# Where the gated output bias is added: four matmuls per group, or GpSimd on the residual rows

## The chip, the cores and the metric

One core of one Trainium2 chip. The metric is the device time of one execution in microseconds (us); lower is better. All times of operations are read from one profiled execution.

## What is computed

A gated cross-attention block, followed by a mixture of eight experts, on 4 x 1024 rows of width 256:

```
x = x + tanh(g_xattn) * (attention(layernorm(x), ctx) @ w_proj.T + b_proj)
x = x + tanh(g_ffn)   * experts_top2(layernorm(x))
```

The attention has 16 heads of 64 and a context of 64 rows; its result is multiplied by the queries ahead of the projection. `b_proj` is a vector of 256. The change concerns only how `tanh(g_xattn) * b_proj` gets into the first line. The experts (two of eight for each row) read what the first line gives.

## The kernel before

The program has two blocks with a barrier between them: `attention` (about the first 357 us of the span) and `experts`.

**Attention.** The 4096 rows are handled in 8 groups of 512 (NG = 8), each as four tiles of 128 rows (TG = 4), and each group in 8 steps, one for each pair of heads (NP = 8). The steps are a software pipeline written out by hand: every engine has its own `step`, and at step n = 8g + p TensorE does the queries of pair n, the scores of n-1, the transposes of the probabilities of n-4, probabilities times values of n-5 and the output projection of n-6; the other engines do what lies between. So the projection of the last pair of group g-1 is done in step 5 of group g (`project_out`, L644), and its result is added to the residual rows in step 6 of group g (`residual`, L1033, VectorE: `xres = pj_ps * gains + xres`, 128x1024 elements). `gains` is tanh(g)/64, because the weights of the projection are held 64 times too large (WS = 64) as two float16 parts, high and low.

**The bias.** At the start ScalarE and VectorE make `bias_rows`, a 128x256 float16 tile that is zero but for row 0 (64 times the bias, high part) and row 32 (its low part): L938, L786 to L788, L992. For the last pair of each group, TensorE multiplies it with a tile of ones (L659), once per tile of rows: four matmuls of 256 columns per group, 32 in all, accumulated in the same PSUM as the projection.

**Order within a step.** What the prediction speaks of, by engine. TensorE ends step 5 with the first transposes of the next group's normalized rows (`x_transpose`, L547). From group 2 to group 6 these wait for the semaphore `pos_read`, since they use the bank `job_ps` that `pick_rows` (L250, VectorE) reads last. VectorE does the routing of group g-2 in steps 3 to 5 of group g, in the gaps between its attention work: logits, best experts, masks (L229), `delta` (L232), `mboth` (L237), positions, `next_row` (L250). In the last group `early_table` (L1069 to L1101) lies between these too. `expert_lo` (L1067) splits an eighth of one expert's weights per step, behind ScalarE's `expert_hi` (L867). ScalarE normalizes the next group's rows in steps 4 and 5 (`ln1_apply`, L765). GpSimd does, in each step: `normalize` (L1300, output `pn`), small powers or the start of a scatter of the routed rows (L1278, L1314, L1316), then `product_lo` (L1306, output `r_l`), which waits for ScalarE's `r_h` (L832). At the end of the last group LAST = 6 more steps drain the pipeline. There VectorE makes the last two `r_l` itself (L1247) and the rest of a table of blocks (L1112 to L1123).

**Residual rows.** SyncE loads group g's rows of x into `xres[g % 2]` (L467) once the rows of g-2 are stored; the issues lie at 42.2 us for group 0, 55.2 for group 1, 274.6 for group 6 and 316.2 for group 7. `residual` waits for that load.

**Last group.** `residual` of group 7 is done in the experts part, at L1638.

**Experts.** 71 blocks of 128 gathered rows, each through two float16 split matmuls (L1483, L1496), TensorE busy nearly throughout. Nothing of it is changed.

Of the kernel before, what the change touches and what calls it, by code (L numbers as in the profile page):

```python
# [22 lines left out]
F32 = mybir.dt.float32  # L23
F16 = mybir.dt.float16
U32 = mybir.dt.uint32
I32 = mybir.dt.int32
ACT = mybir.ActivationFunctionType
ALU = mybir.AluOpType
AX = mybir.AxisListType

P = 128
B, L, D = 4, 1024, 256
# [4 lines left out]
NP = H // 2  # L37
TG = 4
G = TG * P
NG = T // G  # L40
# [4 lines left out]
WS = 64.0  # L45
# [224 lines left out]
def attention(nc, ctx, dram, carry, weights):  # L270
    ident = carry.ident
    gate_t, ones, before, iota_e, tok_ids, minus_half = (
        carry.gate_t, carry.ones, carry.before, carry.iota_e, carry.tok_ids, carry.minus_half)
    pad_rec, gains, wait_mark = carry.pad_rec, carry.gains, carry.wait_mark
# [4 lines left out]
    def sb(name, shape, dt):  # L279
        return ctx.enter_context(nc.sbuf_tensor(name, shape, dt))  # L280
# [4 lines left out]
    def sem(name):  # L285
        return ctx.enter_context(nc.semaphore(name))
# [3 lines left out]
    wp_h, wp_l = (sb(f"wp_{s}", [P, NP, D], F16) for s in "hl")  # L290
    kb = sb("kb", [P, B, NP, 2 * M], F32)
    vb = sb("vb", [P, B, NP, 2, DK], F32)
    bias_rows = sb("bias_rows", [P, D], F16)
    bias_high = sb("bias_high", [64, D], F16)
    tanhs = sb("tanhs", [P, 2], F32)

    stage = sb("stage", [P, WN], F32)
    split = sb("split", [P, 2, WN], F16)
    bias_sb = sb("bias_sb", [64, D], F32)  # L300

    xin = sb("xin", [P, 2, TG, D], F32)
    xres = carry.x1
# [45 lines left out]
    pj_ps = carry.pair_ps  # L350
# [4 lines left out]
    gain_in, gate_in, bias_in, ctx_in, wk_in, wv_in, wp_in = (sem(n) for n in (  # L355
        "gain_in", "gate_in", "bias_in", "ctx_in", "wk_in", "wv_in", "wp_in"))
# [6 lines left out]
    xres_in = [sem(f"xres_in{i}") for i in range(2)]  # L363
# [1 line left out]
    x1_stored = sem("x1_stored")  # L365
    base_set, consts_set, k_zeroed, setup_ops, tanh_done, first_rows = (sem(n) for n in (
        "base_set", "consts_set", "k_zeroed", "setup_ops", "tanh_done", "first_rows"))
    wp_hi, wp_lo, wq_hi, wq_lo, bias_hi = (sem(n) for n in ("wp_hi", "wp_lo", "wq_hi", "wq_lo", "bias_hi"))
    bias_zeroed, bias_lo = sem("bias_zeroed"), sem("bias_lo")
    k_mm, k_placed, v_mm, v_placed = (sem(n) for n in ("k_mm", "k_placed", "v_mm", "v_placed"))  # L370
    ln1_ops, ln1_rstd, ln1_shift, xn_done, xt_tp, xt_hi, xt_lo = (sem(n) for n in ("ln1_ops", "ln1_rstd", "ln1_shift", "xn_done", "xt_tp", "xt_hi", "xt_lo"))
    last_r_lo = sem("last_r_lo")
# [2 lines left out]
    e_sum, e_inv, p_nrm, ot_mm, r_mul, r_hi, r_lo, pj_mm = (sem(n) for n in (  # L375
        "e_sum", "e_inv", "p_nrm", "ot_mm", "r_mul", "r_hi", "r_lo", "pj_mm"))
# [10 lines left out]
    def pair_no(g, p):  # L387
        return g * NP + p

    def known(g, least):  # L390

        return not isinstance(g, int) or g >= least
# [45 lines left out]
    def _(sp):  # L438
# [1 line left out]
        sp.dma_start(xin[:, 0, TG // 2:TG], x_groups[0][:, TG // 2:TG]).then_inc(x_in[0], 16)  # L440
        sp.dma_start(ctx_t, dram["ctxt"]).then_inc(ctx_in, 16)
        sp.dma_start(wk_sb, dram["wk"]).then_inc(wk_in, 16)
        sp.dma_start(bias_sb[:, :], dram["bproj"].partition_broadcast(64)).then_inc(bias_in, 16)
        sp.dma_start(wv_sb, dram["wv"]).then_inc(wv_in, 16)
        sp.dma_start(wp_sb, dram["wproj"]).then_inc(wp_in, 16)
        sp.dma_start(gate_t[:, :, :], dram["gate"]).then_inc(gate_in, 16)
# [93 lines left out]
    def _(pe):  # L540
# [103 lines left out]
        def project_out(g, n, p):  # L644
            pe.wait_ge(r_hi, n + 1)
            if isinstance(n, int) and n == 0:
                pe.wait_ge(v_placed, B)
                pe.wait_ge(bias_hi, 2)
                pe.wait_ge(bias_lo, 1)
                pe.wait_ge(consts_set, CONSTS)  # L650
            if p == 0:
                after(pe, x1_done, g)
            for t in range(TG):
                for i, wt in enumerate((wp_h, wp_l)):

                    nc.tensor.matmul(pj_ps[:, t, :], r_h[:, p % 2, t * P:(t + 1) * P], wt[:, p, :],  # L656
                                     start=(p == 0 and i == 0 and t % 2 == 0), stop=False, skip_group_check=True)
                if p == NP - 1:
                    nc.tensor.matmul(pj_ps[:, t, :], ones[:, :], bias_rows[:, :], start=False, stop=False, skip_group_check=True)  # L659
            if isinstance(n, int) and n >= NS - 2:  # L660
                pe.wait_ge(last_r_lo, n - NS + 3)
            else:
                pe.wait_ge(r_lo, n + 1)
            for t in range(TG):
                last = nc.tensor.matmul(pj_ps[:, t, :], r_l[:, p % 2, t * P:(t + 1) * P], wp_h[:, p, :],
                                        start=False, stop=(p == NP - 1), skip_group_check=True)
            last.then_inc(pj_mm, 1)
# [75 lines left out]
        for p in range(LAST):  # L743
            n = NS + p
# [9 lines left out]
    def _(act):  # L754
# [27 lines left out]
            split_wq(half)  # L782
        for k in range(KD):
            split_x(0, 0, k, first_banks[k])
        act.wait_ge(bias_in, 16)
        nc.scalar.mul(bias_high[:, :], bias_sb[:, :], WS).then_inc(bias_hi, 1)  # L786
        act.wait_ge(bias_zeroed, 1)
        nc.scalar.mul(bias_rows[0:1, :], bias_sb[0:1, :], WS).then_inc(bias_hi, 1)  # L788

        def place_k(p):  # L790

# [130 lines left out]
        for p in range(LAST):  # L922
            n = NS + p
# [11 lines left out]
    @block.vector  # L935
    def _(dve):
        nc.vector.memset(kb[:, 0:B // 2].rearrange("p b n m -> p (b n m)").bitcast(U32), 0).then_inc(k_zeroed, 1)
        nc.vector.memset(bias_rows[:, :].bitcast(U32), 0).then_inc(bias_zeroed, 1)  # L938

        def ln1(g, par):  # L940

# [45 lines left out]
        for k in range(KD):  # L987
            split_x(0, 0, k, first_banks[k])
        split_wq(1)
        dve.wait_ge(bias_hi, 1)  # L990
        dve.wait_ge(bias_zeroed, 1)
        nc.vector.scalar_tensor_tensor(bias_rows[32:33, :], bias_sb[32:33, :], WS, bias_high[32:33, :],  # L992
                                       ALU.mult, ALU.subtract).then_inc(bias_lo, 1)

        def place_k(p):

# [36 lines left out]
        def residual(g, par):  # L1033

            dve.wait_ge(pj_mm, pair_no(g, NP))
            dve.wait_ge(xres_in[par], 16 * (g // 2) + 16 if isinstance(g, int) else g)
            nc.vector.scalar_tensor_tensor(xres[par][:, :, :], pj_ps[:, :, :], gains[:, 0:1], xres[par][:, :, :],
                                           ALU.mult, ALU.add).then_inc(x1_done, 1)

# [165 lines left out]
            last.then_inc(ln1_ops, 1)  # L1205

        def residual_of(b, g, k):
            if isinstance(b, int):
                residual(g - 1, 1 - k)
                return  # L1210
            par = 1 - k
            dve.wait_ge(pj_mm, pair_no(g - 1, NP))
            dve.wait_ge(xres_in[par], (b + k) * 16)
            nc.vector.scalar_tensor_tensor(xres[par][:, :, :], pj_ps[:, :, :], gains[:, 0:1], xres[par][:, :, :],
                                           ALU.mult, ALU.add).then_inc(x1_done, 1)

        for k in range(GB):
            for p in range(NP):
                step(0, k, k, p, pairs_back=min(LAST, k * NP + p))
            if k == 0:  # L1220
                dve.wait_ge(tanh_done, 1)
                nc.vector.tensor_scalar(carry.halves[:, 0:1], tanhs[:, 1:2], 0.5 / WS, None, ALU.mult)
                nc.vector.tensor_scalar(carry.halves[:, 1:2], tanhs[:, 1:2], -0.5 / WS, None, ALU.mult)
                nc.vector.tensor_scalar(gains[:, :], tanhs[:, :], 1.0 / WS, None, ALU.mult).then_inc(setup_ops, 1)
                dve.wait_ge(setup_ops, 1)
# [7 lines left out]
        for p in range(LAST):  # L1233
            n = NS + p
# [24 lines left out]
    def _(pool):  # L1259
# [43 lines left out]
        def product_lo(n, p):  # L1303

            pool.wait_ge(r_hi, n + 1)
            nc.gpsimd.tensor_tensor(r_l[:, p % 2, :], r32[:, p % 2, :], r_h[:, p % 2, :], ALU.subtract).then_inc(r_lo, 1)  # L1306

        def scatter(g, par, i):

            if i == 0:  # L1310
                pool.wait_ge(routed.slots_done, g + 1)
                pool.wait_ge(rec_done, g + 1)

                nc.gpsimd.tensor_tensor(wait_mark[:, 1:2], wait_mark[:, 0:1], wait_mark[:, 0:1], ALU.add)  # L1314
            c, t = i // TG, i % TG
            pool.indirect_dma_start(records, bass.IndirectOffsetOnAxis(slot[par][:, c, t:t + 1], 0),  # L1316
                                    rec[par][:, c, t, :], None).then_inc(records_in[par], 16)

        def step(g, k, p, pairs_back=LAST):
            n = pair_no(g, p)  # L1320
            if pairs_back >= 3:
                normalize(n - 3, (p - 3) % NP)
            if p == 3 and has_next(g):
                ln_rstd(0, g + 1, ln1_ops, ln1_rstd)
            if p == 7 and known(g, 1) and has_next(g):
                ln_rstd(1, g - 1, ln2_ops, ln2_rstd)
            if p >= 5 and known(g, 2):
                scatter(g - 2, k, p - 5)
            if p < 5 and known(g, 3):
                scatter(g - 3, 1 - k, p + 3)  # L1330
            if pairs_back >= 5:
                product_lo(n - 5, (p - 5) % NP)

        for g in range(GB + 1):
            for p in range(NP):
# [12 lines left out]
        for p in range(NP):  # L1348
            step(NG - 1, 1, p)
        for p in range(3):  # L1350
            normalize(NS + p - 3, NP + p - 3)
            product_lo(NS + p - 5, NP + p - 5)
        pool.wait_ge(records_in[0], 16 + 32 * TG * (B - 1))
        pool.wait_ge(records_in[1], 16 + 32 * TG * (B - 2) + 16 * (2 * TG - LEFT))

# [442 lines left out]
```

## Time and profile before

| What | us |
|---|---|
| Median of 3 runs | 764.19 (764.18 to 774.77) |
| The profiled execution, its own time | 762.03 |
| Its span, first to last instruction | 760.3 |
| TensorE busy in the span | 728.7 |
| VectorE busy | 584.4 |
| ScalarE busy | 377.3 |
| GpSimd busy | 371.3 |

In the profile PE is TensorE's matmuls, PEld its weight loads, DVE VectorE, ACT ScalarE, POOL GpSimd. A row of the timeline gives the start and the duration in us, the engine, the line, output<-inputs and the shape; in square brackets stands the idle time of the engine just before it and what ended that. Matmuls are pipelined, and their listed durations overlap: the distance of two starts is what one costs. L12 is line 12 of the kernel. The granted TensorE clock was 0.997 of full speed in the mean.

### The profile page before, as it was taken

To read this page: it belongs to the slowest core of one execution; us is meant where nothing else is said; L and a number is where in the kernel's file an instruction comes from. 1 tells how busy PE (TensorE), PEld (TensorE's weight loads), DVE (VectorE), ACT (ScalarE), POOL (GpSimd) and SP (SyncE) were. 2 spreads that over 40 slices of the span, in tenths; PEclk is the share of its full clock that TensorE was granted. 3 is DMA by queue.
4 is the path that set the end of the run, shared out by engine and by line. 5 is a ranking of instruction groups with operands and counts; after the bars stand their busy time and mean duration, and the time that the engine had idled before them with its cause. 6 is when DMAs were issued, how large, how long until landed. Compare 5 with 4: busy or idle time off the path is not lost.

```text
span 760.3 us, 23505 instructions
## 1 busy us (share of the span) xinstructions
PE 728.7 (96%) x7980; PEld 605.1 (80%) x7981; DVE 584.4 (77%) x1270; ACT 377.3 (50%) x671; POOL 371.3 (49%) x308
## 2 busy tenths in 40 slices
PE   7999999999999999998899999999999999999994
PEld 6567777767677776666789988899999999999994
DVE  5788879798897989796778868767767676767761
ACT  3686676777677667754344422233333333333331
POOL 5135445766676766674424647433343433334332
PEclk9999999999999999999999999999999999999998
DMA  8452443536282725433888875433334333333422
GB/s 302 152 153 98 153 153 131 175 132 216 72 284 77 250 85 197 130 121 111 248 219 215 233 203 103 67 49 48 52 45 55 43 54 48 49 53 45 57 33 26
DMA packets 93177, 93.88 MB, mean 123 GB/s; under 512 B 59312, under 2 KB 77936, under 8 KB 92720
## 3 DMA queue, kind: packets, MB, share of 16 engines
q1 hardware_dynamic: 31184, 64.97, 25.3%
q0 software_dynamic: 13392, 18.03, 13.7%
q10 hardware_dynamic: 48528, 9.92, 7.5%
q8 instruction: 43, 0.70, 0.4%
q14 instruction: 30, 0.25, 0.1%
HBM read 53.89 MB, written 37.95 MB: 121 GB/s over the span
## 4 chain that ended last, share of the span: by engine, by line
PE 39%; DMA 7%; issue 3%; POOL 2%; ACTq 1%; ACT 0%; DVE 0%; POOLq 0%; DVEq 0%
PE h_ps L1483 20%; PE pair_ps L1496 18%; DMA out<-y,meta 7%; POOL records L1742 1%; POOL out L1736 1%; ACTq L158 0%; ACT y L1555 0%; ACTq L160 0%; POOLq L141 0%; PE h_ps L1527 0%; DVE bx_l L1614 0%; POOL last_rstd L1748 0%; ACT bx_h L1543 0%; DVE ht_h L1626 0%; DVE w_now L1620 0%
## 5 line engine op out<-in xcount | busy, mean ns | idle before, releaser
L1736 POOL DMA_INDIRECT out<-y,meta x71 | 132.6, 1868 | 222.5 <-ACT y L1555 191.0
L1483 PE MATMUL h_ps<-bx_h,w_now 128*128 128x128 f16 x2272 | 194.5, 219 | 5.9 <-DVE bx_l L1614 4.5
L1496 PE MATMUL pair_ps<-weights,ht_h 128*128 x1136 | 190.7, 273 | 1.8 <-issue 1.2
L1483 PEld LDWEIGHTS h_ps<-bx_h,w_now 128*128 128x128 f16 x2272 | 152.4, 98 | 11.2 <-DVE bx_l L1614 6.5
L1483 PE MATMUL h_ps<-bx_l,w_now 128*128 128x128 f16 x1136 | 156.2, 219 | 0.5 <-issue 0.5
L1496 PE MATMUL pair_ps<-weights,ht_l 128*128 x568 | 154.8, 273 | 0.0
L1496 PEld LDWEIGHTS pair_ps<-weights,ht_h 128*128 128x128 f16 x1136 | 110.2, 97 | 17.1 <-issue 2.6
L1555 ACT ACTIVATE y<-pair_ps,meta 128x256 f32<-128x256 f32 x71 | 33.7, 474 | 169.3 <-DVE meta L1609 85.2
L1626 DVE CAST ht_h<-hid 128x1024 f16<-128x1024 f32 x71 | 49.7, 700 | 80.9 <-ACT hid L1548 79.7
L1306 POOL TENSOR_TENSOR r_l<-r,r_h 128x512 f16<-128x512 f32 x62 | 75.3, 1214 | 73.7 <-ACT r_h L832 71.8
L1548 ACT ACTIVATE hid<-h_ps 128x1024 f32<-128x1024 f32 x71 | 72.6, 1022 | 63.9 <-PE h_ps L1483 63.1
L1628 DVE TENSOR_TENSOR ht_l<-hid,ht_h 128x1024 f16<-128x1024 f32 x71 | 87.0, 1225 | 2.4
L1483 PEld LDWEIGHTS h_ps<-bx_l,w_now 128*128 128x128 f16 x1136 | 87.2, 98 | 0.0
L1620 DVE COPY w_now<-weights 128x4096 f16 x71 | 84.8, 1194 | 0.2 <-DVE loads_base L1644 0.2
L1300 POOL TENSOR_TENSOR pn<-ex,rinv 128x512 f32<-128x512 f32 x64 | 66.5, 1039 | 30.4 <-DVE rinv L1024 30.4
L614 PEld LDWEIGHTS s_ps<-kb,q 128*128 128x128 f32 x512 | 67.1, 191 | 9.3 <-issue 0.7
L614 PE MATMUL s_ps<-kb,q 128*128 128x128 f32 x512 | 67.5, 275 | 0.3 <-DVE ssub L1015 0.3
L656 PE MATMUL pair_ps<-wp_h,r_h 128*128 128x256 f16 x256 | 61.3, 275 | 0.8 <-ACT r_h L832 0.8
L656 PE MATMUL pair_ps<-wp_l,r_h 128*128 128x256 f16 x256 | 60.7, 273 | 0.0
L1496 PEld LDWEIGHTS pair_ps<-weights,ht_l 128*128 128x128 f16 x568 | 55.6, 98 | 5.2
L1010 DVE TENSOR_REDUCE smax<-s_ps 128x8 f32<-128x512 f32 x64 | 43.1, 674 | 17.8 <-PE s_ps L614 17.1
L821 ACT COPY e<-pt_ps 128x512 f32<-128x512 f32 x64 | 37.4, 584 | 36.0 <-PE pt_ps L625 36.0
(250 smaller groups left out, 1236.5 us busy)
## 6 DMA issues: line engine op xcount, KB each, us to landing
stage<-in_w SPq DMA_DIRECT2D x16, 1024.0 KB
w_split<-split SPq DMA_DIRECT2D x14, 1024.0 KB, 6.5
weights<-w_split SPq DMA_DIRECT2D x14, 1024.0 KB
rows<-records ACTq DMA_DIRECT2D x268, 32.0 KB
xin<-in_x SPq DMA_DIRECT2D x7, 512.0 KB, 5.5
x_even<-in_x SPq DMA_DIRECT2D x4, 512.0 KB
x_odd<-in_x SPq DMA_DIRECT2D x4, 512.0 KB
out<-x_even SPq DMA_DIRECT2D x4, 512.0 KB
```

The costliest lines, as they stand in the source:

```text
L614: last = nc.tensor.matmul(s_ps[:, t].rearrange("p h m -> p (h m)"), q32[:, p, t * P:(t + 1) * P], kb[:, b, p, :] if isinstance(b, int) els ...
L656: nc.tensor.matmul(pj_ps[:, t, :], r_h[:, p % 2, t * P:(t + 1) * P], wt[:, p, :], start=(p == 0 and i == 0 and t % 2 == 0), stop=False, sk ...
L1010: nc.vector.tensor_reduce(smax[:, p % 2], s_ps[:, :, :, :], AX.X, ALU.max).then_inc(s_max, 1)
L1300: nc.gpsimd.tensor_tensor(pn[:, p % 2].rearrange("p h t m -> p t h m"), ex[:, p % 2].rearrange("p t (h m) -> p t h m", h=2), rinv[:, p % 2 ...
L1306: nc.gpsimd.tensor_tensor(r_l[:, p % 2, :], r32[:, p % 2, :], r_h[:, p % 2, :], ALU.subtract).then_inc(r_lo, 1)
L1483: last = nc.tensor.matmul(h_ps[r % 2][:, c, :], w1_now[:, r % 2, s, k * F + c * P:k * F + c * P + P], xt[:, r % 2, k, :], start=(j == 0 an ...
L1496: last = nc.tensor.matmul(y_ps[r % 2], ht[:, r % 2, c, :], weights_at(e, s, WN // 2 + c * D, D).rearrange("p o n -> p (o n)"), start=(c == ...
L1548: nc.scalar.activation(hid[:, r % 2], h_ps[r % 2][:, :, :], ACT.Silu, scale=1.0 / WS).then_inc(h_act, 1)
L1620: nc.vector.tensor_copy(w1_now[:, r % 2], weights[:, bass.ds(e, 1), :, 0:KD * F].rearrange("p o s n -> p (o s) n")).then_inc(w1_ready, 1)
L1626: nc.vector.tensor_copy(ht_h[:, r % 2], hid[:, r % 2]).then_inc(h_hi, 1)
L1628: nc.vector.tensor_tensor(ht_l[:, r % 2], hid[:, r % 2], ht_h[:, r % 2], ALU.subtract).then_inc(h_lo, 1)
L1736: pool.indirect_dma_start(out, bass.IndirectOffsetOnAxis(meta[:, r, 0:1].bitcast(U32), 0), y[:, r % 2, :], None, compute_op=ALU.add).then_ ...
```

## The change

The matmuls with `bias_rows`, and what prepares that tile, go. The bias is loaded as float32 on all 128 partitions (before: 64), VectorE multiplies it once by tanh(g_xattn), at the end of group 0, and GpSimd adds it to the residual rows in place, one tile of 128x256 at the end of each of steps 1 to 4 of the next group, and four tiles in a row at the very end for group 7. VectorE's `residual` waits for these adds in place of the load.

```diff
-    bias_rows = sb("bias_rows", [P, D], F16)
-    bias_high = sb("bias_high", [64, D], F16)
+    bias = sb("bias", [P, D], F32)
-    bias_sb = sb("bias_sb", [64, D], F32)
...
-        sp.dma_start(bias_sb[:, :], dram["bproj"].partition_broadcast(64)).then_inc(bias_in, 16)
+        sp.dma_start(bias[:, :], dram["bproj"].partition_broadcast(P)).then_inc(bias_in, 16)
...
-                pe.wait_ge(bias_hi, 2)
-                pe.wait_ge(bias_lo, 1)
...
-                if p == NP - 1:
-                    nc.tensor.matmul(pj_ps[:, t, :], ones[:, :], bias_rows[:, :], start=False, stop=False, skip_group_check=True)
...
-        act.wait_ge(bias_in, 16)
-        nc.scalar.mul(bias_high[:, :], bias_sb[:, :], WS).then_inc(bias_hi, 1)
-        act.wait_ge(bias_zeroed, 1)
-        nc.scalar.mul(bias_rows[0:1, :], bias_sb[0:1, :], WS).then_inc(bias_hi, 1)
...
-        nc.vector.memset(bias_rows[:, :].bitcast(U32), 0).then_inc(bias_zeroed, 1)
...
-        nc.vector.scalar_tensor_tensor(bias_rows[32:33, :], bias_sb[32:33, :], WS, bias_high[32:33, :],
-                                       ALU.mult, ALU.subtract).then_inc(bias_lo, 1)
...
         def residual(g, par):
 
             dve.wait_ge(pj_mm, pair_no(g, NP))
-            dve.wait_ge(xres_in[par], 16 * (g // 2) + 16 if isinstance(g, int) else g)
+            dve.wait_ge(bias_added, TG * (g + 1))
...
             if k == 0:
                 dve.wait_ge(tanh_done, 1)
+                dve.wait_ge(bias_in, 16)
+                nc.vector.tensor_scalar(bias[:, :], bias[:, :], tanhs[:, 0:1], None, ALU.mult).then_inc(bias_scaled, 1)
...
+        def add_bias(g, t):
+
+            if t == 0:
+                pool.wait_ge(xres_in[g % 2], 16 * (g // 2) + 16)
+                pool.wait_ge(bias_scaled, 1)
+            nc.gpsimd.tensor_tensor(xres[g % 2][:, t, :], xres[g % 2][:, t, :], bias[:, :], ALU.add).then_inc(bias_added, 1)
...
             if pairs_back >= 5:
                 product_lo(n - 5, (p - 5) % NP)
+            if 1 <= p <= TG and known(g, 1):
+                add_bias(g - 1, p - 1)
...
         for p in range(3):
             normalize(NS + p - 3, NP + p - 3)
             product_lo(NS + p - 5, NP + p - 5)
+        for t in range(TG):
+            add_bias(NG - 1, t)
```

## Rows read from the trace of the kernel before

**Rows 1.** One stretch: busy us (instructions) of PE, PEld, DVE, ACT, POOL; PEclk, DMA, GB/s.

```profile
190.00:230.00 40.00, 39.02 (x335) 28.09 (x333) 34.95 (x96) 27.78 (x52) 27.32 (x27) 1.00 0.50 169
```

**Rows 2.** Groups of instructions by line and shape, from 0 to 370 us.

```profile
L659 PE MATMUL pair_ps<-bias_rows,ones 128*128 128x256 f16 x32 | 8.7, 273 | 0.0
...
L1300 POOL TENSOR_TENSOR pn<-ex,rinv 128x512 f32<-128x512 f32 x64 | 66.5, 1039 | 30.4 <-DVE rinv L1024 30.4
...
L1278 POOL TENSOR_TENSOR rstd<-vare,minus_half 128x4 f32<-128x4 f32 x14 | 14.5, 1034 | 16.0 <-DVE vare L1056 12.1 <-DVE vare L957 3.9
...
L1314 POOL TENSOR_TENSOR wait_mark<-wait_mark 128x1 f32<-128x1 f32 x6 | 1.2, 193 | 13.6 <-DVE tok_ids L267 13.6
```

**Rows 3.** Timeline of TensorE, step 5 of one group (start, duration, us).

```profile
162.40 0.27 PE L659 MATMUL pair_ps<-bias_rows,ones 128*128 128x256 f16 x1
...
162.51 0.27 PE L656 MATMUL pair_ps<-wp_h,r_h 128*128 128x256 f16 x1
...
163.17 0.60 PE L665 MATMUL pair_ps<-wp_h,r_l 128*128 128x256 f16 x4
...
164.56 0.75 PE L547 MATMUL job_ps<-ident,xn 128*128 128x128 f32 x4 [0.80 <-DVE next_row L250]
```

**Rows 4.** Who waited for whom, TensorE, 70 to 350 us (us, times, longest).

```profile
PE job_ps L547 <- DVE next_row L250: 4.0, 5, 0.8
```

**Rows 5.** Timeline, the routing operations of steps 3 to 5 of that group.

```profile
151.54 0.69 DVE L1010 TENSOR_REDUCE smax<-s_ps 128x8 f32<-128x512 f32 x1 [1.62 <-PE s_ps L614]
...
154.36 0.67 DVE L1067 SCALAR_TENSOR_TENSOR split<-stage,split 128x512 f16<-128x512 f32 x1
...
154.63 1.57 POOL L1306 TENSOR_TENSOR r_l<-r,r_h 128x512 f16<-128x512 f32 x1 [1.27 <-ACT r_h L832]
...
154.95 0.22 DVE L229 TENSOR_TENSOR mask<-iota_e,best_at 128x64 f32<-128x64 f32 x1
...
155.08 1.14 DVE L232 TENSOR_TENSOR delta<-best 128x4 f32<-128x4 f32 x1
...
160.58 0.69 DVE L1067 SCALAR_TENSOR_TENSOR split<-stage,split 128x512 f16<-128x512 f32 x1 [1.08 <-ACT split L867]
...
164.35 0.16 DVE L250 TENSOR_TENSOR next_row<-job_ps,next_row 128x8 f32<-128x8 f32 x1
```

**Rows 6.** Timeline, step 5 of group 1.

```profile
80.30 1.08 ACT L765 ACTIVATE xn<-xin,shift,rstd 128x256 f32<-128x256 f32 x2
...
81.53 0.65 PE L547 MATMUL job_ps<-ident,xn 128*128 128x128 f32 x4
```

**Rows 7.** Timeline, step 3 of the last group.

```profile
322.09 1.12 DVE L232 TENSOR_TENSOR delta<-best 128x4 f32<-128x4 f32 x1
...
323.15 0.21 DVE L1082 TENSOR_TENSOR cum<-upto,full 1x64 f32<-1x64 f32 x1
```

**Rows 8.** Timeline, last step of the last group.

```profile
338.97 0.68 DVE L1030 TENSOR_TENSOR r<-ot_ps,q 128x512 f32<-128x512 f32 x1
...
339.08 0.62 ACT L867 ACTIVATE split<-stage 128x512 f16<-128x512 f32 x1
```

**Rows 9.** Timeline, the end of the attention part.

```profile
348.81 1.16 POOL L1306 TENSOR_TENSOR r_l<-r,r_h 128x512 f16<-128x512 f32 x1 [0.67 <-ACT r_h L832]
...
351.22 0.69 DVE L1247 TENSOR_TENSOR r_l<-r,r_h 128x512 f16<-128x512 f32 x1 [0.68 <-ACT r_h L832]
...
351.83 0.35 DVE L1112 TENSOR_TENSOR past<-block_no,full_ends 1x200 f32<-1x200 f32 x1
...
355.31 0.60 PE L665 MATMUL pair_ps<-wp_h,r_l 128*128 128x256 f16 x4
...
356.20 0.16 DVE L1123 CAST table<-blk_e 1x25 int32<-1x25 f32 x1
```

**Rows 10.** Timeline of VectorE, the wait for the second group's rows of x.

```profile
21.95 1.40 DVE L944 BATCH_NORM_STATS2 stats<-xin 128x6 f32<-128x256 f32 x4 [4.30 <-DMA xin<-in_x]
```

**Rows 11.** One stretch of the start, columns as in rows 1.

```profile
5.00:10.00 5.00, 4.23 (x26) 4.04 (x25) 2.64 (x12) 2.11 (x2) 1.71 (x8) 1.00 1.03 405
```

More of the change, by code:

```diff
@@ L367, in attention @@
         "base_set", "consts_set", "k_zeroed", "setup_ops", "tanh_done", "first_rows"))
-    wp_hi, wp_lo, wq_hi, wq_lo, bias_hi = (sem(n) for n in ("wp_hi", "wp_lo", "wq_hi", "wq_lo", "bias_hi"))
-    bias_zeroed, bias_lo = sem("bias_zeroed"), sem("bias_lo")
+    wp_hi, wp_lo, wq_hi, wq_lo = (sem(n) for n in ("wp_hi", "wp_lo", "wq_hi", "wq_lo"))
+    bias_scaled, bias_added = sem("bias_scaled"), sem("bias_added")
     k_mm, k_placed, v_mm, v_placed = (sem(n) for n in ("k_mm", "k_placed", "v_mm", "v_placed"))
@@ L989, in _ @@
         split_wq(1)
-        dve.wait_ge(bias_hi, 1)
-        dve.wait_ge(bias_zeroed, 1)
-        nc.vector.scalar_tensor_tensor(bias_rows[32:33, :], bias_sb[32:33, :], WS, bias_high[32:33, :],
-                                       ALU.mult, ALU.subtract).then_inc(bias_lo, 1)
         def place_k(p):
@@ L1207, in residual_of @@
         def residual_of(b, g, k):
[L1208 to L1215, printed above, removed]
+            residual(g - 1, 1 - k)
         for k in range(GB):
```

## The prediction

> **What bounds the kernel.** I read the table of stretches first, then the groups of instructions, the table of waits, and the timeline step by step. The stretch of 40 us in the main loop shows TensorE busy 39.0, VectorE 35.0, ScalarE 27.8 and GpSimd 27.3 [rows 1]. TensorE looks like the bound, so less TensorE work should pay. The removed work is small, though: 32 matmuls [rows 2]. Their 273 ns is a pipelined duration; the next matmul starts 0.11 us later [rows 3], so they cost 32 x 0.11 = 3.5 us, 0.44 us for each group and 0.5% of the run. (A measurement of this kernel tells about 2%, 15 us, from no change.) GpSimd gains 32 adds.
>
> What matters is where the 0.44 us lies. All four matmuls of a group are in step 5. The last projection matmuls of that step start at 163.17 and are issued by 163.17 + 4 x 0.11 = 163.61. The transposes behind them start only at 164.56, released by VectorE's `next_row` [rows 3]. This wait stands five times in the table of waits, 0.8 us each [rows 4], once in each of groups 2 to 6. Counted from the issue it is 0.95 us.
>
> What makes `next_row` late is a chain that begins in step 3. VectorE waits there for the scores (151.54, idle 1.62), then works without a gap of its own through the routing operations, waits for ScalarE's part of the weight split (160.58), and reaches `next_row` at 164.35 to 164.51 [rows 5]. In this chain no instruction waits for the projection of step 5. So the piece from step 3 to step 5 is set by VectorE and ScalarE, and the rest of the group by TensorE.
>
> **Removed, part by part.** Groups 2 to 6: TensorE reaches its wait 0.44 us sooner and waits 1.39 us in place of 0.95. Gain 0; the cover is gone only if `next_row` came 0.44 us sooner too.
> Group 1 has no such wait, but its transposes need the rows that ScalarE normalizes at 80.30 to 81.38, and start at 81.53 [rows 6]. With the 0.05 us that a release takes (164.51 to 164.56 in rows 3 and 5), they could start at 81.43. Gain 0.1, not 0.44.
> Group 7 has no transposes in step 5. There TensorE does run ahead by 0.44, but VectorE has no recorded idle time from 318 to 344 us, and the drain hangs on its products. It waits for others only by little: `expert_lo` of the last step starts as ScalarE's part ends, at 339.08 + 0.62 = 339.70, where VectorE itself was free at 338.97 + 0.68 = 339.65, or some 0.1 earlier, as its operations overlap [rows 8]. Gain 0.15 (0 to 0.44).
> The drain: the last four matmuls lie ahead of TensorE's end at 355.31 + 0.60 = 355.91, but VectorE ends at 356.36 with the table [rows 9], and the barrier waits for both. Gain 0.
> The waits and small operations of the start end long before anyone needs them, at 12.6 to 15.1 us, ahead of waits for other things. Gain 0. Sum of the gains: 0.25 us of 3.5.
>
> **The price of an add.** No 256-column add is in the trace. A 512-column product of two float32 tiles takes 1039 ns and a 1-column add 193 ns [rows 2]: linear in between, 193 + 255 x (1039 - 193)/511 = 615 ns. The bounds are 0.19 and 1.04 us (the power on 4 columns takes 1.03 too, another function). I take 0.615; the start-to-start distance is then about 0.58. 32 adds are some 19 us of GpSimd, 2.5 us per group of 41.6 us.
>
> **What is queued behind it.** Behind each add stands the next step's `normalize`. In the traced groups it starts 0.58 later in steps 2, 3 and 5, and not at all later in step 4, where it waits for VectorE anyway. TensorE transposes `pn` in the step after, so 2.5 us and more of slack cover it. `product_lo` waits for `r_h` and comes no later. `residual` comes more than a step behind the fourth add, and the loads land a step or more before the first. Cost in these places 0; if an add took over 2 us, TensorE would wait.
>
 It speaks against this change, since GpSimd adds are not free beside VectorE; by it a waiting `delta` would go ahead of an add that starts later.
>
> I went through the two-SBUF operations that the adds, or what they shift, would meet:
> - `delta`, groups 2 to 6. It already waits for `r_l`; now an add stands right behind `r_l`. If `delta`, which asked first, gets the port, it costs 0; if GpSimd keeps it, 0.58 each, directly on the chain to `next_row`, so 5 x 0.58 = 2.9 us. No row shows VectorE waiting where GpSimd has a second instruction ready. I take 0: the mask at 154.95 went ahead of an `r_l` that had waited since 154.63, so the port is given up between instructions.
> - the variance of step 2: its 0.15 us operation meets the shifted `normalize` and loses up to 0.6, but VectorE idles 1.62 us before step 3's scores [rows 5]. 0.
> - group 7, step 3: behind `delta` comes a further two-SBUF operation of the table, 323.15 [rows 7]. It meets the add: 0 if it follows `delta` unbroken, as the mask did, 0.58 if not. I take 0.3, as nothing decides.
> - the drain. `r_l` ends at 348.81 + 1.16 = 349.97; the four adds then fill 349.93 to about 352.3. VectorE's own `r_l` at 351.22 and the table operation at 351.83 [rows 9] read two SBUF tiles each. The first waits for the end of the third add, about 351.7, hence 0.5. The second follows unbroken (0) or behind the fourth add (0.6 more). All later VectorE work, to the end at 356.36, shifts with them. I take 0.6, bounds 0.45 and 1.2.
>
> **The start.** The wider load of the bias moves 64 KB more in a stretch that runs at 405 GB/s [rows 11]: 0.16 us. It stands ahead of the rows of group 1, which VectorE waits for until 21.95 [rows 10]. I take 0.16, bounds 0 and 0.4. The scaling of the bias (one 128x256 operation, under 0.5 us) falls at 54.7 us, and VectorE idles for TensorE a few steps later. 0.
>
> **Sum.** -0.25 + 0.3 + 0.6 + 0.16 = +0.8 us on the profiled execution: span 760.3 to 761.1, own time 762.03 to 762.8. The median of the runs shown is 2.2 above that own time, so I carry the difference over to it: 764.19 + 0.8 = 765.0. The experts part starts 0.8 later and is otherwise the same.
>
> **Rivals.**
> 1. TensorE is the bound and all 3.5 us come back: 760.7, or with the drain's 0.6 given back, 761.3. For it speaks the 39.0 of 40 us; against it the five waits of 0.8 us [rows 4], which take what is removed before them. It needs `next_row` to come sooner, and nothing in the change does that. Chance 0.1.
> 2. Slower: GpSimd keeps the port from `r_l` to the add, and `delta` waits 0.58 longer in groups 2 to 7. This lies on the chain that TensorE waits for. Five groups are 2.9 us, and the last takes 0.58 in place of my 0.3: 765.0 + 2.9 + 0.3 = 768.2. It decides as soon as a waiting VectorE loses to a queued GpSimd instruction. Against it stands the mask's case. Chance 0.2.
> 3. The add is far dearer than a line through two rows gives, up to 1.04 us: the drain then loses up to 2 us in place of 0.6, group 7 0.5 more, and the shifted `normalize` of step 2 and 3 stays within slack: 764.19 + 0.8 + 1.4 + 0.3 = 766.7. Chance 0.1.
>
> My forecast has 0.6. The range leaves out rival 1 at its full size (one in ten), takes in a gain of part of it, and reaches over rival 2 by 0.6: 761.5 to 768.8. Over 2% either way would need 15 us; the whole of the removed work is 3.5, and an add that cost its full 0.6 us every time would be 19. Faster 0.01, same 0.98, slower 0.01.
>
> **What would show it.** TensorE's wait for `next_row` grows from 0.8 to about 1.2 us in groups 2 to 6, and the distance of two `residual` operations stays 41.6 us. Adds of 0.6 us, some longer where `expert_lo` or `delta` holds the port. `delta` stays at 1.15 us (1.7 would be rival 2). `r_l` of VectorE in the drain takes 1.1 to 1.2 us in place of 0.69, and the barrier comes about 0.9 later against the end of the main loop. If the distance of two residuals falls to 41.2 us, the cover that I name is not there and I am wrong.

## The result, and the profile after

| | before | after |
|---|---|---|
| median of 13 runs | 764.19 us (761.65 to 774.77) | 767.95 us (765.52 to 771.46) |
| own time of the profiled execution | 762.03 us | 771.46 us |
| its span | 760.3 us | 769.7 us |

The ratio is 1.0038, with a 95% interval of 1.0022 to 1.0055. On 764.19 us that is +2.9 us (1.7 to 4.2). It is within 2%, and inside the predicted range, but the interval leaves out both zero and my +0.8 us. The removed TensorE work brought nothing, and something else cost about 3 us.

The profiled execution after the change happens to be the longest of its 13 runs, so its whole span isn't the thing to compare. I cut both executions at two instructions that both have: the first `residual`, and the first matmul of the experts part. The timeline of TensorE after the change, at that second mark:

```profile
359.78 1.39 PE L1518 MATMUL h_ps<-before,ones 128*128 128x128 f16 x22 [1.85 <-PEq L138]
```

Before the change this instruction starts at 357.32. The first `residual` starts at 82.54 before and at 82.03 after. So the piece between them (I call it the attention length) is 274.78 us before and 277.75 after: **+2.97 us**. The experts part behind it is 402.98 and 409.92 us. The runs as a whole don't carry the 6.9 us more there: by its ratio the change costs 2.9 us in all, and the attention length alone has 2.97. In this one execution a stretch ran at half the clock. (Over the nine profiled executions of this study the experts part takes 401.9 to 403.6 us in the three kernels with the bias matmuls and 405.1 to 409.9 in the six without, and in each of the six the granted clock falls once between 440 and 505 us. Why is not shown.) The busy time by stretches, after:

```profile
365.00:370.00 5.00, 2.39 (x35) 1.83 (x31) 3.78 (x6) 1.77 (x3) 2.34 (x3) 0.94 0.70 182
370.00:375.00 5.00, 4.70 (x23) 3.38 (x24) 4.08 (x14) 0.58 (x1) 0.00 (x0) 0.50 0.94 273
375.00:380.00 5.00, 5.00 (x65) 4.72 (x64) 2.15 (x4) 1.79 (x3) 2.87 (x2) 0.88 0.56 149
```

The granted clock is 0.50 (1.2 GHz) between 370 and 375, and in the 5 us before TensorE had been busy for 2.39. In the same piece before the change it was busy for 2.64 of 5 us and the clock stayed at 1.00.

**Where the 2.97 us lie.** The distances of two `residual` operations, in us:

| | 1-2 | 2-3 | 3-4 | 4-5 | 5-6 | 6-7 | last one to the experts |
|---|---|---|---|---|---|---|---|
| before | 41.25 | 41.56 | 41.58 | 41.56 | 41.57 | 42.02 | 25.24 |
| after | 41.68 | 41.99 | 41.99 | 42.00 | 42.00 | 42.35 | 25.74 |

Each of the first five grows by 0.41 to 0.44, the sixth by 0.33, the end by 0.50: 2.47 + 0.50 = 2.97. The 0.43 us of a group stands in the table of waits of TensorE, 70 to 350 us, where [rows 4] had 4.0, 5, 0.8:

```profile
PE job_ps L545 <- DVE next_row L250: 8.3, 5, 1.7
```

I had said that the wait would grow to about 1.2 (0.80 + 0.44) and the distance stay. It grew to 1.67. So `next_row` is 0.43 us late in each of groups 2 to 6. The timeline of VectorE after the change, the stretch that [rows 5] ends with:

```profile
162.60 0.69 DVE L1000 TENSOR_TENSOR ssub<-s_ps,smax 128x512 f32<-128x512 f32 x1
163.21 0.71 DVE L258 TENSOR_SCALAR rec_odd<-lean,halves 128x4 f32<-128x4 f32 x1
163.83 0.28 DVE L259 TENSOR_SCALAR rec_odd<-lean,halves 128x4 f32<-128x4 f32 x1
164.03 0.16 DVE L260 CAST rec_odd<-tok_ids 128x8 uint32<-128x8 f32 x1
164.10 0.68 DVE L1015 TENSOR_TENSOR r<-ot_ps,q 128x512 f32<-128x512 f32 x1
164.70 0.15 DVE L250 TENSOR_TENSOR next_row<-job_ps,next_row 128x8 f32<-128x8 f32 x1
```

and that of GpSimd:

```profile
161.06 1.15 POOL L1286 TENSOR_TENSOR r_l<-r,r_h 128x512 f16<-128x512 f32 x1 [1.81 <-ACT r_h L822]
162.17 0.72 POOL L1293 TENSOR_TENSOR x_even<-x_even,bias 128x256 f32<-128x256 f32 x1
162.85 1.04 POOL L1280 TENSOR_TENSOR pn<-ex,rinv 128x512 f32<-128x512 f32 x1
```

The same place before the change, VectorE and GpSimd:

```profile
162.26 1.03 POOL L1300 TENSOR_TENSOR pn<-ex,rinv 128x512 f32<-128x512 f32 x1
...
163.30 0.28 DVE L258 TENSOR_SCALAR rec_odd<-lean,halves 128x4 f32<-128x4 f32 x1
163.49 0.28 DVE L259 TENSOR_SCALAR rec_odd<-lean,halves 128x4 f32<-128x4 f32 x1
```

L258 is the first of two small operations that scale the record's weights. It reads one tile, four columns. Before the change it starts at 163.30, and `pn` has ended at 162.26 + 1.03 = 163.29: just clear, by 0.01 us (as in all of groups 2 to 6; in group 7 by 0.10). After the change the fourth add stands ahead of `pn`, which now runs to 162.85 + 1.04 = 163.89. L258 starts at 163.21 and ends at 163.92, just behind `pn`. It takes 0.71 in place of 0.28. Everything behind it on VectorE moves by 0.43, `next_row` too, and TensorE waits for that. In group 7 L258 takes 0.62, which is the 0.33 us of the sixth distance.

**The end of the attention part**, GpSimd and VectorE after the change, which answers to [rows 9]:

```profile
351.85 3.37 POOL L1293 TENSOR_TENSOR x_odd<-x_odd,bias 128x256 f32<-128x256 f32 x4
...
353.14 0.69 DVE L1227 TENSOR_TENSOR r_l<-r,r_h 128x512 f16<-128x512 f32 x1 [0.68 <-ACT r_h L822]
353.75 0.88 DVE L1097 TENSOR_TENSOR past<-block_no,full_ends 1x200 f32<-1x200 f32 x1
...
358.66 0.16 DVE L1108 CAST table<-blk_e 1x25 int32<-1x25 f32 x1
```

The table operation takes 0.88 where it took 0.35: +0.53, and the end comes 0.50 later. VectorE's `r_l` takes its old 0.69, though it reads two SBUF tiles and stands among the adds. Here GpSimd is the one that waits: two adds in a row take 1.41 us in experiment 6, so four would take about 2.8, and these take 3.37.

### The profile page after: what moved, and what is told of

It is laid out like the page before. It is cut to its first block, busy times and chain, and to the rows that moved or that the text cites. A ratio compares the mean times of both kernels' runs of the same rounds, so it can differ in the third digit from the quotient of the medians.

```text
span 769.7 us, 23477 instructions
## 1 busy us (share of the span) xinstructions
PE 730.3 (95%) x7948; PEld 605.8 (79%) x7949; DVE 588.8 (76%) x1269; ACT 376.7 (49%) x669; POOL 388.9 (51%) x340
## 4 chain that ended last, share of the span: by engine, by line
PE 45%; issue 3%; DVE 2%; DMA 1%; DVEq 0%; ACTq 0%; ACT 0%; POOLq 0%
PE h_ps L1474 23%; PE pair_ps L1487 22%; DMA out<-y,meta 1%; DVE ht_h L1617 0%; DVE w_now L1611 0%; DVEq L1428 0%; DVE bx_l L1605 0%; ACTq L158 0%; POOLq L141 0%; PE last_job_ps L1505 0%; PE h_ps L1518 0%; ACT y L1546 0%; PE last_job_ps L190 0%; DVE meta L1600 0%; DVE bx L165 0%
## 5 line engine op out<-in xcount | busy, mean ns | idle before, releaser
L1487 PE MATMUL pair_ps<-weights,ht_h 128*128 x1136 | 193.0, 275 | 1.7 <-issue 1.1
L1474 PEld LDWEIGHTS h_ps<-bx_h,w_now 128*128 128x128 f16 x2272 | 154.1, 98 | 13.4 <-DVE bx_l L1605 8.4
```

Of the source, the lines that this page charges most:

```text
L1474: last = nc.tensor.matmul(h_ps[r % 2][:, c, :], w1_now[:, r % 2, s, k * F + c * P:k * F + c * P + P], xt[:, r % 2, k, :], start=(j == 0 an ...
L1487: last = nc.tensor.matmul(y_ps[r % 2], ht[:, r % 2, c, :], weights_at(e, s, WN // 2 + c * D, D).rearrange("p o n -> p (o n)"), start=(c == ...
```

## The experiments

The experiments test this theory: removing the four matmuls is worth 0 in the groups; the shift of `pn` by the fourth add holds L258 and costs 0.43 us per group; the four adds at the end cost 0.5. The rivals: the adds themselves load something shared (memory, or the port in other places); or the removal of the matmuls changed the order in some way that costs. All lengths below are from the profiled executions, and the ratios are to the kernel before.

**1. The adds one step earlier.** The adds of a group stand in steps 0 to 3 in place of 1 to 4, so none is ahead of the `pn` that meets L258.

```
-            if 1 <= p <= TG and known(g, 1):
-                add_bias(g - 1, p - 1)
+            if p < TG and known(g, 1):
+                add_bias(g - 1, p)
```

> The four adds of a group move from steps 1 to 4 to steps 0 to 3; same number, same size. Theory A (the loss comes from one place: the fourth add pushes `pn` of step 5 by 0.7 us, so that it still holds the port when VectorE's `tensor_scalar` of the record weights, L258, wants it): that operation is back at 0.28 us, two residuals are 41.6 us apart in place of 42.0, the ratio to the kernel before is 1.0005 (0.5 us left, from the drain). Theory B (each add costs, wherever it stands): nothing changes, 42.0 us and a ratio of 1.004.

The timeline around L258, GpSimd and VectorE:

```profile
160.76 1.03 POOL L1280 TENSOR_TENSOR pn<-ex,rinv 128x512 f32<-128x512 f32 x1
...
161.80 0.28 DVE L258 TENSOR_SCALAR rec_odd<-lean,halves 128x4 f32<-128x4 f32 x1
```

`pn` ends at 161.79 and L258 starts at 161.80, as before the change. The distances are 41.26, 41.55, 41.58, 41.56, 41.57, 42.02, those of before. The attention length is 275.28, +0.50, and all of this is the end (25.74). The ratio is 1.0015 (0.9995 to 1.0036). So 2.47 of the 2.97 us come from where the add stands.

**2. No matmuls and no adds.** All calls of `add_bias` are left out; `residual` waits for its rows as before. The bias is left out of the output.

> The bias is left out altogether: no matmuls and no adds, the rest as in the changed kernel. It shows what the removed 3.5 us of TensorE are worth alone. Theory A (TensorE would only wait longer for `next_row`): the wait is about 1.2 us by the profile's count in groups 2 to 6, the residuals 41.6 us apart, ratio 0.9995 to 1.000. Rival (TensorE is the bound): 41.2 us apart, 3 us less, ratio 0.996.

The attention length is 274.74 (-0.04), the distances are 41.25, 41.58, 41.55, 41.57, 41.57, 42.01, the end 25.21. The wait for `next_row`:

```profile
PE job_ps L545 <- DVE next_row L250: 6.2, 5, 1.2
```

It is 1.24 each, the 0.80 + 0.44 of the prediction. So the removed 3.5 us of TensorE are worth 0 here, in a kernel where nothing was added. The ratio is 1.0017 (1.0000 to 1.0033). With an unchanged attention part I would have expected 1.000; its experts part took 405.6 us, and I can't say whether anything but the scatter of that part is behind it.

**3. The adds, and the matmuls too.** The kernel before, with a tile of zeros that GpSimd adds as in the change; `residual` waits for the adds, as there.

```
+        nc.gpsimd.memset(bias[:, :], 0.0).then_inc(bias_scaled, 1)
...
+            if 1 <= p <= TG and known(g, 1):
+                add_bias(g - 1, p - 1)
...
+        for t in range(TG):
+            add_bias(NG - 1, t)
```

> The kernel before, bias matmuls and all, with GpSimd's 32 adds on top at the places of the change; they add a tile of zeros. It shows what the adds cost alone. Theory A: as much as the change itself, since the matmuls cost nothing: residuals 42.0 us apart, L258 at 0.7 us, ratio 1.003 to 1.004. Rival (the matmuls' 3.5 us were gained and the adds cost 6): ratio 1.008.

The same place in the timeline of this kernel:

```profile
162.56 0.72 POOL L1316 TENSOR_TENSOR x_even<-x_even,bias 128x256 f32<-128x256 f32 x1
163.24 1.03 POOL L1303 TENSOR_TENSOR pn<-ex,rinv 128x512 f32<-128x512 f32 x1
...
163.60 0.70 DVE L258 TENSOR_SCALAR rec_odd<-lean,halves 128x4 f32<-128x4 f32 x1
```

`pn` ends at 164.27, L258 at 164.30. The attention length is 277.75, to the hundredth that of the change. The ratio is 1.0046 (1.0027 to 1.0065). So the adds are the whole loss, and the matmuls, present or not, change nothing in the attention part. The wait for `next_row` is 1.22 here: the 0.8 of before and the 0.43 of the hold, without the 0.44 of the removal.

**4. Another operation in that place.** The change, with the two scalings of the weights moved behind `next_row`. The copy of the token numbers (eight 32-bit elements per partition) stayed ahead, and so it now stands where L258 stood. The text on record speaks as if nothing that can be held were left there.

```
+def record_tokens(nc, carry, rec):
...
                 if gap == 2:
-                    record_weights(nc, dve, route, routed, carry, g - 2, rec[k])
+                    record_tokens(nc, carry, rec[k])
                 if gap == 3:
                     pick_rows(nc, dve, job_ps, route, routed, carry, g - 2)
                 if gap == 4:
+                    record_weights(nc, dve, route, routed, carry, g - 2, rec[k])
```

> The changed kernel, with the two `tensor_scalar` of the record weights (L258, L259) issued behind `pick_rows` and the weight split, just ahead of `row_numbers`, in place of ahead of `times_q`; adds as in the change. Theory A: they no longer meet `pn` and no longer stand ahead of `next_row`, which comes 0.8 us sooner (0.7 + 0.1 of start-to-start); two residuals are 41.2 us apart, the time is 4 us below the changed kernel's, ratio 0.998 to 0.999 to the kernel before. Theory B: only the order changes, 0.4 us per group at most, ratio 1.001.

The expectation (41.2 us, ratio 0.998 to 0.999) was wrong, in a useful way. The same place in the timeline:

```profile
161.63 1.04 POOL L1285 TENSOR_TENSOR pn<-ex,rinv 128x512 f32<-128x512 f32 x1
...
161.99 0.71 DVE L264 CAST rec_odd<-tok_ids 128x8 uint32<-128x8 f32 x1
...
164.02 0.28 DVE L258 TENSOR_SCALAR rec_odd<-lean,halves 128x4 f32<-128x4 f32 x1
```

The copy takes 0.71 in place of 0.16 and ends at 162.70, again 0.03 behind the end of `pn` (162.67), while L258, moved away, is back at 0.28. So the hold goes with the place, and both single-input operations are held. Four of the distances are 41.72 to 41.75: about 0.17 over before, as the hold of 0.55 stands against 0.38 of work that no longer lies ahead of `next_row`. The first distance, 41.80, has the hold alone (+0.55): the moved work still stands ahead of every group's `residual`, so that an earlier `next_row` pays only behind it, in the next distance. The sixth is 42.09 (+0.07) and the end 25.74, that of the change. The attention length is 276.57, +1.79. The ratio is 1.0021 (0.9997 to 1.0045).

**5. `next_row` first, in the kernel before.** If TensorE waits for `next_row`, the cheapest cure is to compute it sooner. Here `next_row`, the copy and the product of the masks stand ahead of `r`, and the scalings of the weights behind.

```
                 if gap == 2:
-                    record_weights(nc, dve, route, routed, carry, g - 2, rec[k])
-                if gap == 3:
-                    pick_rows(nc, dve, job_ps, route, routed, carry, g - 2)
+                    pick_rows(nc, dve, job_ps, route, routed, carry, g - 2, rec[k])
                 if gap == 4:
+                    record_weights(nc, dve, route, routed, carry, g - 2, rec[k])
```

> The kernel before (bias by matmuls, no adds), with VectorE's order in step 5 changed: `next_row` stands ahead of `times_q` and of the record weights; the weights come last, the copy of the token numbers right behind `next_row`. Theory A (the period is set by VectorE's chain to `next_row`, not by TensorE): `next_row` comes about 1.1 us sooner, TensorE's transposes then wait only for ScalarE's rows `xn` (by the trace of before 163.63, against 164.56), so two residuals are 40.6 to 40.8 us apart and 4 to 4.5 us are gained in groups 2 to 6, ratio 0.994 to 0.995. Rival (TensorE is the bound, the waits are harmless): 41.6 us apart, ratio 1.000.

TensorE's timeline around the transposes:

```profile
162.59 0.27 PE L665 MATMUL pair_ps<-bias_rows,ones 128*128 128x256 f16 x1
162.69 0.60 PE L671 MATMUL pair_ps<-wp_h,r_l 128*128 128x256 f16 x4
163.31 0.72 PE L553 MATMUL job_ps<-ident,xn 128*128 128x128 f32 x4
```

The transposes no longer wait for `next_row`: it ends at 163.00, and ScalarE's rows `xn`, the other thing that they need, at 163.16. The distances after the first are 40.89 to 40.91 (the last 41.33), some 0.67 less each; the first stays at 41.26, for the reason given in experiment 4. The attention length is 271.44, -3.34, where I had expected 4 to 4.5; the difference stays open. The median of 7 runs is 759.77 against 765.02, ratio 0.9947 (0.9917 to 0.9976).

**6. The same order in the kernel after**, with the adds in steps 0 to 3, and at the end two of the four adds put between the last `normalize` and `product_lo` operations.

```
             normalize(NS + p - 3, NP + p - 3)
+            if p != 1:
+                add_bias(NG - 1, p // 2)
             product_lo(NS + p - 5, NP + p - 5)
-        for t in range(TG):
+        for t in range(2, TG):
             add_bias(NG - 1, t)
```

> The changed kernel with the same order on VectorE, the adds of a group in steps 0 to 3, and two of group 7's four adds between `normalize` and `product_lo` of the drain. Theory A: the same distance as the sister run with the matmuls, 40.6 to 40.8 us, as ScalarE's rows come last in both; the removed matmuls are worth nothing here either, and the drain loses 0 to 0.3 us in place of 0.5. Ratio 0.994 to 0.995. Rival (with the chain shortened, TensorE's 0.44 us per group come back): 40.3 us, ratio 0.992.

The timeline of TensorE at the transposes, and of GpSimd and VectorE at the end of the attention part:

```profile
161.51 0.60 PE L665 MATMUL pair_ps<-wp_h,r_l 128*128 128x256 f16 x4
162.56 0.72 PE L551 MATMUL job_ps<-ident,xn 128*128 128x128 f32 x4 [0.45 <-ACT xn L765]
...
346.00 1.41 POOL L1298 TENSOR_TENSOR x_odd<-x_odd,bias 128x256 f32<-128x256 f32 x2
...
347.90 0.35 DVE L1103 TENSOR_TENSOR past<-block_no,full_ends 1x200 f32<-1x200 f32 x1
```

The attention length is 271.41 (-3.37), the distances are those of experiment 5 to the hundredth or two, the end is 25.21. With adds that end at 346.00 + 1.41 = 347.41 the table operation is back at 0.35, so the 0.5 us of the end is the adds' place too. And the four matmuls of a group are worth nothing a second time: the 0.44 us that TensorE saves it spends waiting for ScalarE's normalized rows (0.44 to 0.45 each time). The ratio is 0.9960 (0.9941 to 0.9979), median 762.21. Experiments 5 and 6 ran on the same chip and both beat both originals; their intervals overlap, so they aren't told apart by the time.

**7. Is it the four columns?** The change, with L258 and its twin each cut in four operations of one column.

```
-    nc.vector.tensor_scalar(rec[:, 0, :, D + 1], r.lean[:, :], ...)
+    for t in range(TG):
+        nc.vector.tensor_scalar(rec[:, 0, t:t + 1, D + 1], r.lean[:, t:t + 1], ...)
```

> The changed kernel, its two `tensor_scalar` of the record weights cut into eight of one column each (128x1 in place of 128x4); the adds and `pn` stay where they are. If the hold comes from how an operation of several float32 elements with one SBUF input is run, the eight take 0.15 us each beside `pn`, and the hold moves to the copy of the token numbers behind them if `pn` still runs, 0.1 us or none; residuals 41.7 to 41.8 us apart. If any VectorE operation with SBUF input and output is held, the first of the eight takes 0.7 us as L258 does, and the distance is 42.1 us or more. One look, told by the trace and not by the time.

The same place in the timeline (a line with x4 groups four instructions):

```profile
164.09 1.04 POOL L1282 TENSOR_TENSOR pn<-ex,rinv 128x512 f32<-128x512 f32 x1
...
164.45 0.81 DVE L259 TENSOR_SCALAR rec_odd<-lean,halves 128x1 f32<-128x1 f32 x4
165.17 0.81 DVE L261 TENSOR_SCALAR rec_odd<-lean,halves 128x1 f32<-128x1 f32 x4
165.90 0.17 DVE L262 CAST rec_odd<-tok_ids 128x8 uint32<-128x8 f32 x1
```

`pn` runs from 164.09 to 165.13, over the whole first four, and none of them waits: each takes 0.25 to 0.27, and they follow one another by 0.18. Here no one-column operation is held. (I had expected 0.15 us for each, and so a distance of 41.7 to 41.8.) It is no cure, since eight of them take 1.45 us where the two took 0.82 with the hold. The second distance is 42.63, the change's 41.99 and these 0.63. The third to the fifth are 44.3, and the clock says why (busy time by stretches, a long one and two short ones in it):

```profile
90.00:165.00 75.00, 71.82 (x618) 51.15 (x618) 65.13 (x182) 53.48 (x99) 48.97 (x50) 1.00 0.42 146
190.00:310.00 120.00, 112.73 (x923) 79.82 (x925) 102.01 (x283) 78.54 (x145) 83.62 (x85) 0.96 0.42 145
...
250.00:255.00 5.00, 3.06 (x30) 2.11 (x28) 4.66 (x16) 3.88 (x9) 2.84 (x3) 1.00 0.00 0
255.00:260.00 5.00, 4.63 (x20) 3.11 (x21) 3.79 (x10) 1.80 (x3) 3.35 (x4) 0.66 0.36 138
```

The 0.96 is a mean and no level. The granted clock is 1.00 throughout, but in each of groups 3 to 6 it falls once to 0.50, for about 3.4 us, and 44.3 - 42.6 = 1.7 us is what a fall costs. Each begins right behind TensorE's wait for `next_row`:

```profile
255.37 0.88 PE L547 MATMUL job_ps<-ident,xn 128*128 128x128 f32 x4 [2.31 <-DVE next_row L250]
```

The edit lengthened that wait from 1.67 to 2.31 us. Behind the 1.67 of the change, in its attention part, the clock never fell, behind the 2.31 of this kernel in four groups of five. So the falls may well belong to the edit's price. The one time of this kernel, 780.5 us, contains them and the scatter of the experts part, and how much of it is the price is not shown.

## Why the prediction was right or wrong

**Right: the bound and the removed work.** The cover that I named, TensorE's wait for `next_row`, took all 0.44 us per group: the wait was 1.24 in experiment 2, and experiments 2, 3 and 6 give the removal a worth of 0 (-0.04; nothing against the change; 0.03 against experiment 5). Rival 1 is out.

**Nearly right: group 1 and group 7, 0.25 us of gain.** The transposes of group 1 start at 80.92, 0.06 us behind ScalarE's rows (79.78 + 1.08 = 80.86), where [rows 6] had 0.15. So the 0.1 is there at this place, but no length measured here shows it. The last group's 0.15 didn't come: its distance without adds is 42.01 (experiment 2), against 42.02.

**Right: `delta` costs nothing, and rival 2 is out.** The waiting `delta` went ahead of the add that was ready behind `r_l`. The timeline after the change:

```profile
154.54 1.58 POOL L1286 TENSOR_TENSOR r_l<-r,r_h 128x512 f16<-128x512 f32 x1 [0.51 <-ACT r_h L822]
...
154.99 1.15 DVE L232 TENSOR_TENSOR delta<-best 128x4 f32<-128x4 f32 x1
...
156.07 0.72 POOL L1293 TENSOR_TENSOR x_even<-x_even,bias 128x256 f32<-128x256 f32 x1
```

`delta` ends at 156.14, with `r_l` (156.12), and not with the add (156.79). In the last group the table operation behind `delta` takes 0.21 as before: my 0.3 us there was 0.

**The size of an add.** 0.72 us, not 0.615; the line through a 1-column and a 512-column operation ran 0.1 low. Rival 3 had this sign, but 0.1 us more for an add isn't the cause: experiment 1 has the same adds, at no cost in the groups.

**Right in size, not in the instruction: the end.** 0.50 against 0.6. I had held `r_l` until the third add ended and let the table operation follow unbroken; it was the other way round, 0 on `r_l` and +0.53 on the table operation alone. With the adds elsewhere it is gone (experiment 6).

**Wrong: the list of the operations that an add, or what it shifts, would meet.** The step that failed is "every VectorE operation with two SBUF inputs that meets an add waits for its end", and the list that I drew up by it. L258 reads one SBUF tile, so I didn't look at it, although the forecast itself shifted `pn` in step 5 by 0.58 and called that free because TensorE has slack there. The hold of such an operation is what the six groups lost, 2.47 us, three times my whole sum. With this term, and the others as they were measured, the sum is 0 + 2.47 + 0.50 = 2.97 us, as the attention length shows, against a time that rose by 2.9 by the ratio (1.7 to 4.2).

That 767.95 lies in my range is luck: the range reached to 768.8 for rival 2, which did not happen, and the term that did come was not in it.

By the rows alone I could have bounded it: the line-up of `pn`'s end (163.29) with L258's start (163.30) was in the trace of before. It would have priced six groups at 0 to 0.6 us each, up to 3.6 us. The same trace also shows the hold itself, at the end of group 0, where VectorE scales the gains beside an `r_l`:

```profile
54.33 1.49 POOL L1306 TENSOR_TENSOR r_l<-r,r_h 128x512 f16<-128x512 f32 x1 [2.02 <-ACT r_h L832]
54.72 0.15 DVE L1222 TENSOR_SCALAR halves<-tanhs 128x1 f32<-128x1 f32 x1
54.78 0.15 DVE L1223 TENSOR_SCALAR halves<-tanhs 128x1 f32<-128x1 f32 x1
54.84 1.00 DVE L1224 TENSOR_SCALAR gains<-tanhs 128x2 f32<-128x2 f32 x1
```

The three operations of VectorE read one SBUF tile each. The two of one column take 0.15 us; the one of two columns takes 1.00 and ends at 55.84, where `r_l` ends (55.82). After the change that operation runs clear of `r_l` and takes 0.15. So operations with one SBUF input can be held, and the kernel before had the row that says so.

The Trainium skill had the rest. SBUF — State Buffer, section "SBUF: two separate sides", names two kinds of VectorE operation for the lock: those with two SBUF inputs, which I used, and those that run in a mode with both read ports. VectorE: DVE Perf Modes, section "Mode 2×_2P — use both read ports for one tensor", says that this is the mode of operations with one tensor, out of SBUF, the two ports reading a half each. The runs agree: L258 with four columns and the copy with eight elements take 0.71 us beside `pn`; one column, which can't be halved, takes 0.25 to 0.27 (experiment 7); and two columns are held where one is not, in the rows just shown. That it is this mode is the page's word; the runs show only who is held and who is not.

**Not resolved: the start.** VectorE's wait for the second group's rows ends at 21.42 us, where [rows 10] had 21.95. The first `residual` starts between 81.0 and 82.6 us in the profiled executions with the wider load and at 82.4 to 82.7 in those without, so no cost of the load shows, and 0.16 us couldn't be seen. The scaling of the bias took 1.25 us, not under 0.5: it too has one SBUF input, and the `r_l` beside it ends at 55.31, the scaling at 55.46. The first `residual` is no later for it.

## What to carry to other kernels

Before you value work that is taken from a busy engine, find the wait behind it: 3.5 us of TensorE were worth 0, before a wait for VectorE and, once that was gone, before one for ScalarE. When you put work on GpSimd, follow what it shifts, not only itself: lay the new end of each shifted operation against each VectorE operation on the chain, and count those with a single SBUF input of a few columns as ones that can be held. Where an engine's order sets the chain, try first to move the operation that the others wait for: putting `next_row` ahead of four VectorE operations brought 3.3 us, where taking 3.5 us of work from TensorE brought none.

## What the runs showed that I had not expected

- A VectorE operation of four columns, one SBUF input, was held for 0.43 us by a GpSimd product, and an eight-element copy for 0.55; one-column operations of the same kind were not held, and one of two columns was, in the kernel before.
- What was held ended 0.03 us behind the GpSimd instruction in three kernels (163.92 and 163.89, 164.30 and 164.27, 162.70 and 162.67), so the cost of such a meeting can be estimated from the two timelines beforehand.
- A schedule can be clear by 0.01 us, in five groups of one kernel, and lose 0.43 us in each by an addition on an engine that is busy for 27 of 40 us.
- In one execution the granted clock fell to half for about 3.4 us in each of four groups, right behind a TensorE wait of 2.31 us, and each fall cost 1.7 us, more than the 0.63 us of work that the edit had added. The mean over 120 us, 0.96, hides this; stretches of 5 us show it.
